# A routing table with 64 bytes for each entry, a smaller descriptor scratch, and the last wait on SyncE

## The chip, the core and the metric

The kernel runs on one core of one Trainium2 chip. The metric is the device time of one execution in microseconds (us). The kernel before was timed in three runs: 564.46, 564.67 and 567.79 us, median 564.67. One further execution was profiled; all rows below are from it.

## The reference

A block of a gated cross-attention model. `x` is [8, 256, 256] (eight batches of 256 tokens), the context is [8, 120, 256].

```python
x = x + tanh(g_xattn) * xattn(layernorm(x), ctx, w_q, w_kv, w_out, b_out)   # 16 heads of 64
x = x + tanh(g_ffn)   * ffn(layernorm(x), W1, W2, Wr)

def ffn(x, W1, W2, Wr):                      # 8 experts of 1024 hidden units
    probs = softmax(einsum('btd,ed->bte', x, Wr))
    topk_vals, topk_idx = top_k(probs, 2)
    gate = one_hot-weighted topk_vals / topk_vals.sum()
    h = silu(einsum('btd,efd->btef', x, W1));  y = einsum('btef,edf->bted', h, W2)
    return einsum('bte,bted->btd', gate, y)
```

Only the two experts that a token chooses count, so the kernel computes those alone. It computes in float16 with each operand split in a high and a low part.

## The kernel before

**Two phases share the engines.** The first phase takes the eight batches one after another through attention, second layer norm, router logits and routing. The second phase is the expert part: the 4096 pairs of token and expert are sorted by expert into 39 tiles of 128 rows (`TILES`), and each tile is gathered, multiplied by W1 and W2 of its expert, and added to the output. The first 13 tiles (`EARLY`) depend on the first five batches only, and tiles 0 to 9 are worked while the last batches are still in attention. Tiles 10 to 38 run in a loop of four tiles (`run_tiles`).

**What sets the order.** The order of each engine's work is written out by hand: each engine has a loop over `p` with a fixed list of calls (for GpSimd, called POOL in the rows, `scatter`, `p_low`, `find_rows`, `tile_gather`, `tile_add` and so on). Engines are in step through semaphores alone. A call that waits holds up everything behind it on its engine.

**The routing table.** `table` is a tensor in HBM with 129 blocks of 128 places. A place belongs to a slot of an expert, and holds the token's number and its gate: 2 float32, 8 bytes. It is used in four steps.

1. `constants` on POOL fills `pad` (a piece of SBUF inside the later `w2s`), and `store_pads` on SyncE (SP) copies it to all of `table` with 2 DMAs, so that unused places name a spare row.
2. Per batch, `route` on VectorE (DVE) writes `entry` and `slot`. `scatter` on POOL (L611) issues four indirect DMAs of 128 entries each; each entry is one 8-byte write to HBM at its slot. Eight batches make 32 of them. They count on `scattered`, which `find_rows` waits for, and `route` two batches later.
3. `find_rows` on POOL (L664) gathers 13 blocks after batch 4 and 26 blocks after batch 7 into `found`, one block a partition. `find_T` on TensorE (PE) transposes it, and `row_ids` on DVE makes `row_of` (which row each place of a tile takes) and the gates.
4. `tile_gather` (L678) fetches the 128 rows of a tile, and `tile_add` (L689) adds the tile's result `yt` to `out` with an indirect DMA that accumulates. An addition is issued only after the one before has landed (`y_added`).

**Other transfers.** SP loads the weights of a tile, `w1_tile` (in the rows `w_tile`), 1 MB each, at L454. `store_norm` stores the normalized rows `xn2`, and `norm2` on ScalarE (ACT, L876) waits for the store of the batch before.

**The end.** POOL's last line waits until all 39 additions have landed. Then every engine leaves the program through a closing step, which the rows show as DRAIN and semaphore instructions at L170. SP has only waited for the direct stores to `out`.

Of the kernel before, what the change touches and what calls it, by code (L numbers as in the profile page):

```python
# [36 lines left out]
BLOCKS = T // P  # L37

# [129 lines left out]
def build(nc, x, ctxT, wq, wkv, wo, bo, gx, gf, w1, w2, wr, out, xn2_dram, table, w1_dram):  # L168
    ctx = ExitStack()
    with ctx:  # L170
# [42 lines left out]
        found = sb("found", [P, 2 * P], F32)  # L213
# [55 lines left out]
        entry = [sb(f"entry{i}", [P, NT, TOPK, 2], F32, att) for i in range(2)]  # L269
# [11 lines left out]
        pad = raw[:, 14336:14336 + 2 * P].rearrange("p (r c) -> p r c", c=2)  # L281
# [116 lines left out]
        def _(sp):  # L398
# [69 lines left out]
            def store_pads(b):  # L468
                if b:
                    return  # L470
                sp.wait_ge(const_done, CONSTS)
                sp.dma_start(table_b[0:P, :], pad.rearrange("p r c -> p (r c)")).then_inc(table_in, 16)
                sp.dma_start(table_b[P:P + 1, :], pad[0:1].rearrange("p r c -> p (r c)")).then_inc(table_in, 16)
# [45 lines left out]
            sp.wait_ge(x2_out[1], 16 * (B + 1))  # L519

        @block.gpsimd
        def _(pool):
# [33 lines left out]
            def constants(b):  # L556
                if b:
# [15 lines left out]
                pool.iota(pad[:, :, 0], [[1, P]], base=T, channel_multiplier=0,  # L573
                          allow_small_or_imprecise_dtypes=True).then_inc(const_done, 1)
# [28 lines left out]
            def scatter(b, t):  # L603
                if not 0 <= b < B:
                    return
                if t == 0:
                    pool.wait_ge(route_done, b + 1)
                    if b == 0:
                        pool.wait_ge(table_in, 32)
                for k in range(TOPK):  # L610
                    pool.indirect_dma_start(out=table[:], out_offset=bass.IndirectOffsetOnAxis(slot[b % 2][:, t, k:k + 1], 0),  # L611
                                            in_=entry[b % 2][:, t, k, :], in_offset=None).then_inc(scattered[b % 2], 16)
# [140 lines left out]
            pool.wait_ge(y_added, 16 * TILES)  # L753

        @block.scalar
        def _(act):
# [156 lines left out]
            def split_high(q, i, k):  # L913
# [10 lines left out]
                else:  # L924
# [10 lines left out]
                    elif q < 7:  # L935
                        for j in range(2):
                            act.wait_ge(stats_done[j], 1)
                    else:
                        act.wait_ge(table_in, 32)
# [130 lines left out]
        def _(dve):  # L1070
# [10 lines left out]
            def constants(b):  # L1081
# [3 lines left out]
                nc.vector.tensor_copy(identb[:], ident[:]).then_inc(zero_done, 1)  # L1085
                chain.link(nc.vector.tensor_copy(base[0][:], seg[:]))
# [547 lines left out]
        def _(pe):  # L1634
# [244 lines left out]
            def find_T(b, late):  # L1879
# [5 lines left out]
                f = found[0:n, :].rearrange("t (r c) -> t r c", c=2)  # L1885
# [204 lines left out]
```

## Time and profile before

| what | value |
|---|---|
| median of three runs | 564.67 us |
| profiled execution, first to last instruction (span) | 560.1 us |
| median of the runs less that span | 4.6 us |
| PE, busy share of the span | 88% |
| DVE, ACT, POOL, busy share | 66%, 66%, 65% |
| DMA queues of SP and of POOL, share of 16 DMA engines | 46.7%, 9.5% |
| mean granted TensorE clock | 0.958 of full |

The profiled execution has no time of its own beside its span; the median of the runs stands 4.6 us above that span, which is launch and end outside the instructions. Busy shares are averages: until about 320 us four engines are busy together, after that PE is busy and the others about half of the time. "Idle before" is an engine's idle time ahead of an instruction, with what ended it; "issue" means that the profile shows nothing that it waited for.

### The profile page before, as it was taken

What the parts mean: (1) busy time and instruction counts of PE and PEld (TensorE: products, weight loads), DVE (VectorE), ACT (ScalarE), POOL (GpSimd) and SP (SyncE); (2) the same over time, 40 slices, a digit from 0 to 9 for tenths busy, and PEclk for the clock granted to TensorE, in tenths of its full rate; (3) what the DMA queues carried; (4) which work ended last, traced back from release to release, by engine and by line L of the source; (5) the groups of instructions that cost most, each with busy time, mean ns of one, the idle gap of its engine ahead of it and who ended that gap; (6) DMA issues with size and microseconds to landing.
All of it is one profiled execution on the core that took longest, in us unless ns stands there. A gap on an engine that the chain in (4) does not pass through costs nothing. (4 is left out here: it accounts for less than half of the span.)

```text
span 560.1 us, 17891 instructions
## 1 busy us (share of the span) xinstructions
PE 493.7 (88%) x6630; PEld 438.3 (78%) x6631; DVE 370.2 (66%) x856; ACT 371.3 (66%) x576; POOL 363.9 (65%) x372
## 2 busy tenths in 40 slices
PE   2869799998999999798788997699999999999990
PEld 2757688887888879687567886689898898988980
DVE  5899999898889899699996664343444444343430
ACT  1838999998999899789546674245455464645530
POOL 5466979798989998788978642533544436344531
PEclk9979889999999999999689998799999999999996
DMA  7922506173553625263438598766787877778421
GB/s 286 392 77 84 175 12 219 48 244 59 175 127 119 178 97 168 33 212 73 130 148 201 153 287 145 208 185 186 214 259 201 259 207 232 229 224 244 112 30 17
DMA packets 34846, 93.13 MB, mean 166 GB/s; under 512 B 4967, under 2 KB 24565, under 8 KB 27490
## 3 DMA queue, kind: packets, MB, share of 16 engines
q1 hardware_dynamic: 25634, 81.86, 46.7%
q0 software_dynamic: 8576, 10.30, 9.5%
q8 instruction: 40, 0.66, 0.6%
q10 hardware_dynamic: 576, 0.14, 0.1%
q14 instruction: 20, 0.16, 0.1%
HBM read 74.17 MB, written 18.12 MB: 165 GB/s over the span
## 5 line engine op out<-in xcount | busy, mean ns | idle before, releaser
L689 POOL DMA_INDIRECT out<-yt,row_of x39 | 65.0, 1667 | 115.3 <-DMA out<-yt,row_of 96.5
L1642 PE MATMUL st_bank<-xsT,w_tile 128*128 128x128 f16 x1872 | 114.4, 221 | 4.3 <-issue 3.3
L1480 DVE SCALAR_TENSOR_TENSOR hT<-hf,h_scale,hT 128x512 f16<-128x512 f32 x78 | 58.6, 754 | 88.1 <-ACT hT L974 88.1
L1642 PEld LDWEIGHTS st_bank<-xsT,w_tile 128*128 128x128 f16 x1872 | 109.2, 99 | 7.0 <-issue 5.4
L1642 PE MATMUL o_bank<-w2s,hT 128*128 x936 | 109.9, 274 | 1.2 <-DVE yt L1489 1.1
L1642 PEld LDWEIGHTS o_bank<-w2s,hT 128*128 128x128 f16 x936 | 90.4, 99 | 12.4 <-issue 1.6
L968 ACT ACTIVATE hf<-st_bank,z_scale 128x512 f32<-128x512 f32 x78 | 52.9, 679 | 47.9 <-PE st_bank L1642 40.4
L592 POOL TENSOR_TENSOR pT<-pT 120x512 f16<-120x512 f32 x64 | 77.3, 1221 | 8.0 <-ACT pT L842 7.7
L974 ACT ACTIVATE hT<-hf,h_scale 128x512 f16<-128x512 f32 x78 | 56.3, 722 | 13.1 <-ACT hf L968 4.5
L637 POOL TENSOR_SCALAR stage<-stage,upw 128x512 f32<-128x512 f32 x32 | 55.9, 1748 | 10.5 <-ACT w_hi L941 10.4
L841 ACT ACTIVATE pT<-st_bank,exp_bias,logit_scale 120x512 f32<-120x512 f32 x64 | 50.0, 781 | 12.1 <-PE st_bank L1858 11.6
L842 ACT ACTIVATE pT<-st_bank,exp_bias,logit_scale 120x512 f16<-120x512 f32 x64 | 50.1, 783 | 0.0
L949 ACT ACTIVATE xsT<-max_pair 128x256 f16<-128x256 f32 x39 | 14.9, 382 | 48.8 <-PE max_pair L1896 44.7
L678 POOL DMA_INDIRECT xg<-xn,row_of x39 | 39.8, 1019 | 11.3 <-issue 8.9
L1778 PE MATMUL j_bank<-wos,oT 128*128 128x256 f16 x384 | 45.4, 272 | 0.3 <-DVE oT L1179 0.3
L1642 PE MATMUL o_bank<-v,pT 120*128 120x65 f16 x768 | 35.1, 197 | 11.7 <-DVE o L1367 9.6
L1642 PEld LDWEIGHTS o_bank<-v,pT 120*128 120x128 f16 x768 | 30.3, 99 | 18.2 <-issue 16.2
L611 POOL DMA_INDIRECT table<-entry,slot x32 | 32.9, 1027 | 14.2 <-DVE entry L1324 7.2
L1642 PE MATMUL j_bank<-xnT,wqs 128*128 128x256 f16 x336 | 41.0, 273 | 0.3 <-DVE oT L1179 0.3
L1778 PEld LDWEIGHTS j_bank<-wos,oT 128*128 128x128 f16 x384 | 36.4, 98 | 4.5 <-DVE oT L1179 0.4
L1344 DVE TENSOR_REDUCE max_pair<-max_pair 128x8 f32<-128x960 f32 x32 | 37.0, 1155 | 0.0
L1489 DVE TENSOR_SCALAR yt<-o_bank,gate_y 128x256 f32<-128x256 f32 x39 | 18.9, 483 | 25.4 <-PE o_bank L1642 25.2
(217 smaller groups left out, 966.5 us busy)
## 6 DMA issues: line engine op xcount, KB each, us to landing
w_tile<-w_split SPq DMA_DIRECT2D x39, 1024.0 KB, 5.2
stage<-in_w SPq DMA_DIRECT2D x16, 1024.0 KB, 5.1
w_split<-w_hi SPq DMA_DIRECT2D x8, 512.0 KB, 2.8
w_split<-stage SPq DMA_DIRECT2D x8, 512.0 KB, 3.9
out<-x SPq DMA_DIRECT2D x17, 128.0 KB, 5.4
xin<-in_x SPq DMA_DIRECT2D x8, 256.0 KB, 4.7
w2s<-in_wkv SPq DMA_DIRECT2D x2, 1024.0 KB, 12.2
xres<-in_x SPq DMA_DIRECT2D x16, 128.0 KB
```

The source lines that it names most:

```text
L592: pool.tensor_tensor(pT[g % 2][:, 1, h, :], pT32[:, h, :], pT[g % 2][:, 0, h, :], ALU.subtract).then_inc(pT_low[h], 1)
L637: chain.link(pool.tensor_scalar(chunk, chunk, upw[q % 2][:, i:i + 1], None, ALU.mult))
L678: pool.indirect_dma_start(out=xg[t % XG][:], out_offset=None, in_=xn2_dram[0:rows], in_offset=bass.IndirectOffsetOnAxis(row_of[:, t:t + 1] ...
L689: pool.indirect_dma_start(out=out[0:rows], out_offset=bass.IndirectOffsetOnAxis(row_of[:, t:t + 1], 0), in_=yt[t % XG][:], in_offset=None, ...
L841: nc.scalar.activation(pT32[:, h, :], st_bank[h][0:M, :], ACT.Exp, bias=exp_bias[0:M], scale=logit_scale[0:M])
L842: nc.scalar.activation(pT[g % 2][:, 0, h, :], st_bank[h][0:M, :], ACT.Exp, bias=exp_bias[0:M], scale=logit_scale[0:M]).then_inc(exp_done[h ...
L968: nc.scalar.activation(hf[par][:, cols], z_bank[a][:], ACT.Silu, scale=z_scale[:, bass.ds(t, 1)]).then_inc(silu_done, 1)
L974: nc.scalar.activation(hT[par][:, 0, 4 * a:4 * a + 4, :], hf[par][:, cols].rearrange("p (c n) -> p c n", c=4), ACT.Copy, scale=h_scale[:, ...
L1344: ins = nc.vector.tensor_reduce(both[:, t].rearrange("p (h c) -> p h c", h=2), max_pair[:, :, 0:HP * M].rearrange("p h (c m) -> p h c m", ...
L1480: nc.vector.scalar_tensor_tensor(out=hT[par][:, 1, 4 * a:4 * a + 4, :], in0=hf[par][:, 512 * a:512 * a + 512].rearrange("p (c n) -> p c n" ...
L1642: ins = pe.matmul(out, lhs[i](a), rhs[i](c), start=(i == 0 and a + c == 0), stop=(i == n - 1 and a == 1))
L1778: ins = pe.matmul(dst[:, 0:D], oT[t][:, a, ic, :], wos[:, c, ic, :], start=(ic + a + c == 0), stop=(ic == IC - 1 and a == 1))
```

## The change

A place in `table` grows from 2 to 16 float32 (`ENTRY`), 64 bytes, of which 14 are zero. `entry`, `found` and `pad` grow with it. The scatter now writes whole places of 64 bytes, the two finds read blocks of 8 KB in place of 1 KB. `pad` is 64 rows of half a block (128 x 1024 float32), so `store_pads` needs six DMAs in place of two. Two memsets on DVE zero `entry` once. `pad` now also covers a part of expert 6's weights, so that ACT's split of these waits for the table's fill as that of expert 7 did. The SBUF that POOL's DMA descriptors get shrinks to 8192 bytes of each partition; before, no size was named. And the wait for the last addition moves from POOL's end to SP's end.

```diff
--- before.py
+++ after.py
@@ -35,6 +35,9 @@
 TOPK = 2
 TILES = TOPK * T // P + E - 1
 BLOCKS = T // P
+
+
+ENTRY = 16
 
 XG = 4
 
@@ -210,7 +213,7 @@
         row_of = sb("row_of", [P, TILES], I32)
         gate_y = sb("gate_y", [P, TILES], F32)
         expert_f = sb("expert_f", [P, TILES], F32)
-        found = sb("found", [P, 2 * P], F32)
+        found = sb("found", [P, ENTRY * P], F32)
         by_expert = sb("by_expert", [P, TILES - EARLY, E], F32)
         one_hot = sb("one_hot", [P, TILES - EARLY, E], F32)
 
@@ -266,7 +269,7 @@
         slot_m = chosen
         slot = [sb(f"slot{i}", [P, NT, TOPK], I32, att) for i in range(2)]
         ratio = sb("ratio", [P, 2, NT], F32, att)
-        entry = [sb(f"entry{i}", [P, NT, TOPK, 2], F32, att) for i in range(2)]
+        entry = [sb(f"entry{i}", [P, NT, TOPK, ENTRY], F32, att) for i in range(2)]
         att.close()
 
         xsT = [sb(f"xsT{i}", [P, 2, KC, P], F16) for i in range(2)]
@@ -278,7 +281,7 @@
 
 
         raw = w2s[:].rearrange("p e s c d -> p (e s c d)").bitcast(F32)
-        pad = raw[:, 14336:14336 + 2 * P].rearrange("p (r c) -> p r c", c=2)
+        pad = raw[:, 13824:13824 + ENTRY * P // 2].rearrange("p (r c) -> p r c", c=ENTRY)
         diag5 = raw[:, 14848:14848 + 5 * P // 2].bitcast(BF16).rearrange("p (i n) -> p i n", n=P)
         raw_k, raw_q, raw_v = (raw[:, 2048 * i:2048 * i + 2048].rearrange("p (k n) -> p k n", k=KC) for i in range(3))
         raw_o = raw[:, 6144:8192].rearrange("p (k n) -> p k n", k=IC)
@@ -469,8 +472,12 @@
                 if b:
                     return
                 sp.wait_ge(const_done, CONSTS)
-                sp.dma_start(table_b[0:P, :], pad.rearrange("p r c -> p (r c)")).then_inc(table_in, 16)
-                sp.dma_start(table_b[P:P + 1, :], pad[0:1].rearrange("p r c -> p (r c)")).then_inc(table_in, 16)
+                for h in range(2):
+                    to = table_b[:, h * ENTRY * P // 2:(h + 1) * ENTRY * P // 2]
+                    rows = pad[64 * h:64 * h + 64].rearrange("p r c -> p (r c)")
+                    for g in range(2):
+                        sp.dma_start(to[64 * g:64 * g + 64, :], rows).then_inc(table_in, 16)
+                    sp.dma_start(to[P:P + 1, :], rows[0:1]).then_inc(table_in, 16)
 
             sp.dma_start(xin[:], x_b[0]).then_inc(xin_in, 16)
             sp.dma_start(raw_q, wq).then_inc(raw_in[2], 16)
@@ -517,6 +524,7 @@
                 load_tile(B - 1, t)
             sp.wait_ge(x2_out[0], 16 * B)
             sp.wait_ge(x2_out[1], 16 * (B + 1))
+            sp.wait_ge(y_added, 16 * TILES)
 
         @block.gpsimd
         def _(pool):
@@ -570,8 +578,13 @@
                 pool.memset(sel[:], 0.0).then_inc(pool_chain, 1)
                 chain.n += 3
                 pool.wait_ge(pool_chain, chain.n)
-                pool.iota(pad[:, :, 0], [[1, P]], base=T, channel_multiplier=0,
-                          allow_small_or_imprecise_dtypes=True).then_inc(const_done, 1)
+                for h in range(2):
+                    ins = pool.iota(pad[64 * h:64 * h + 64, :, 0], [[1, 64]], base=T + 64 * h, channel_multiplier=0,
+                                    allow_small_or_imprecise_dtypes=True)
+                    if h == 0:
+                        chain.link(ins)
+                ins.then_inc(const_done, 1)
+                pool.wait_ge(const_done, CONSTS - 2)
                 pool.affine_select(out=upper[:], in_=upper[:], compare_op=ALU.is_gt, fill=0.0, base=0,
                                    pattern=[[1, P]], channel_multiplier=-1).then_inc(const_done, 1)
 
@@ -606,7 +619,7 @@
                 if t == 0:
                     pool.wait_ge(route_done, b + 1)
                     if b == 0:
-                        pool.wait_ge(table_in, 32)
+                        pool.wait_ge(table_in, 96)
                 for k in range(TOPK):
                     pool.indirect_dma_start(out=table[:], out_offset=bass.IndirectOffsetOnAxis(slot[b % 2][:, t, k:k + 1], 0),
                                             in_=entry[b % 2][:, t, k, :], in_offset=None).then_inc(scattered[b % 2], 16)
@@ -750,7 +763,6 @@
                 if t + XG < TILES:
                     gather(t + XG)
                 add(t)
-            pool.wait_ge(y_added, 16 * TILES)
 
         @block.scalar
         def _(act):
@@ -932,11 +944,11 @@
                             act.wait_ge(job_full, JOBS.fulled(name, 0))
                         if piece == 0:
                             act.wait_ge(ctx32_done, 2)
-                    elif q < 7:
+                    elif q < 6:
                         for j in range(2):
                             act.wait_ge(stats_done[j], 1)
                     else:
-                        act.wait_ge(table_in, 32)
+                        act.wait_ge(table_in, 96)
                     to, done = w2_part(q, 0, c, 1024), w2_high[k]
                 nc.scalar.activation(to, stage[i][:, c:c + 1024], ACT.Copy, scale=upw[q % 2][:, i:i + 1]).then_inc(done, 1)
 
@@ -1083,6 +1095,8 @@
                     return
                 dve.wait_ge(ident_done, IDENT)
                 nc.vector.tensor_copy(identb[:], ident[:]).then_inc(zero_done, 1)
+                for i in range(2):
+                    chain.link(nc.vector.memset(entry[i][:], 0.0))
                 chain.link(nc.vector.tensor_copy(base[0][:], seg[:]))
 
             def x_stats(b, part):
@@ -1882,7 +1896,7 @@
                 n = (EARLY, TILES - EARLY)[late]
                 dst = bank_free(FOUND[late], b)
                 pe.wait_ge(found_in, 16 * (1 + late))
-                f = found[0:n, :].rearrange("t (r c) -> t r c", c=2)
+                f = found[0:n, :].rearrange("t (r c) -> t r c", c=ENTRY)
                 pe.transpose(dst[:, 0:n], f[:, :, 0], ident[0:n, 0:n])
                 pe.transpose(dst[:, 64:64 + n], f[:, :, 1], ident[0:n, 0:n]).then_inc(job_full, 1)
 
@@ -2076,13 +2090,13 @@
         "w2": np.asarray(L0_ffn_W2).reshape(E, D, FC, P).transpose(0, 3, 2, 1),
         "wr": np.asarray(L0_ffn_Wr).reshape(E, KC, P).transpose(2, 1, 0),
     }
-    nc = bacc.Bacc("TRN2", target_bir_lowering=False, num_devices=1)
+    nc = bacc.Bacc("TRN2", target_bir_lowering=False, num_devices=1, dynamic_dma_scratch_size=8192)
     arrays = {f"in_{name}": np.ascontiguousarray(layout[name]) for name in INPUTS}
     args = [nc.dram_tensor(f"in_{name}", arrays[f"in_{name}"].shape, F32, kind="ExternalInput").ap() for name in INPUTS]
 
     out = nc.dram_tensor("out", (T + P, D), F32, kind="ExternalOutput").ap()
     xn2_dram = nc.dram_tensor("xn2", (T + P, D), F32, kind="Internal").ap()
-    table = nc.dram_tensor("table", (P * (P + 1), 2), F32, kind="Internal").ap()
+    table = nc.dram_tensor("table", (P * (P + 1), ENTRY), F32, kind="Internal").ap()
     w1_dram = nc.dram_tensor("w1_split", (E, P, 2, KC, DFF), F16, kind="Internal").ap()
     build(nc, *args, out, xn2_dram, table, w1_dram)
     result = run_bass_kernel_spmd(nc, [arrays], core_ids=[0])
```

The order of two engines changes at one place each. SP, at `store_pads`, early in the program (`w2s` is the tensor in which `pad` lies). Before:

```order
L490 DMA xn<-x_1 64x256 x2
L419 DMA xres<-in_x 128x256 x2
L472 DMA table<-w2s 128x256
L473 DMA table<-w2s 1x256
L412 DMA xin<-in_x 128x2x256
```

With the change:

```order
L497 DMA xn<-x_1 64x256 x2
L422 DMA xres<-in_x 128x256 x2
L479 DMA table<-w2s 64x1024 x2
L480 DMA table<-w2s 1x1024
L479 DMA table<-w2s 64x1024 x2
L480 DMA table<-w2s 1x1024
L415 DMA xin<-in_x 128x2x256
```

Six DMAs stand where two stood; the next one behind them, a load of `xin`, is the same.

DVE, at its `constants`, between the scales of the first weights (`pw`, `up`) and the first input (`xn2T`). Before:

```order
L1124 TENSOR_SCALAR pw<-pw 128x1 [waits dve_chain]
L1132 TENSOR_SCALAR up<-pw 128x1 [waits dve_chain]
L1085 CAST identb<-ident 128x128 [waits ident_done]
L1086 COPY base<-seg 128x8
L1200 TENSOR_SCALAR xn2T<-j_bank,up 128x512 [waits up_done2,job_full,dve_chain]
```

With the change:

```order
L1138 TENSOR_SCALAR pw<-pw 128x1 [waits dve_chain]
L1146 TENSOR_SCALAR up<-pw 128x1 [waits dve_chain]
L1097 CAST identb<-ident 128x128 [waits ident_done]
L1099 MEMSET entry 128x64
L1099 MEMSET entry 128x64 [waits dve_chain]
L1100 COPY base<-seg 128x8 [waits dve_chain]
L1214 TENSOR_SCALAR xn2T<-j_bank,up 128x512 [waits up_done2,job_full,dve_chain]
```

Two memsets, each waited for, are put in ahead of the copy to `base`.

## Rows read from the trace of the kernel before

**Rows 1.** Windows: stretch, busy us of PE, PEld, DVE, ACT, POOL, clock, DMA share, GB/s.

```profile
341.00:349.00 8.00, 4.67 (x58) 4.28 (x56) 2.72 (x8) 1.89 (x4) 0.00 (x0) 0.83 0.97 95
351.00:353.00 2.00, 2.00 (x34) 1.94 (x32) 1.27 (x3) 0.00 (x0) 0.64 (x1) 1.00 0.92 348
...
346.20:349.60 3.40, 2.74 (x20) 2.35 (x21) 0.00 (x0) 0.99 (x3) 0.00 (x0) 0.50 0.92 130
```

**Rows 2.** Timeline of POOL, 330 to 360 us: start, us, engine, line, operation, idle before.

```profile
332.73 1.25 POOL L611 DMA_INDIRECT table<-entry,slot  x1 [0.31 <-issue]
...
337.35 0.96 POOL L611 DMA_INDIRECT table<-entry,slot  x1 [0.30 <-issue]
338.61 1.59 POOL L689 DMA_INDIRECT out<-yt,row_of  x1 [0.30 <-issue]
352.36 1.97 POOL L689 DMA_INDIRECT out<-yt,row_of  x1 [12.16 <-DVE yt L1489]
```

**Rows 3.** DMA issues from 332 to 350 us, median us to landing last.

```profile
w_tile<-w_split SPq DMA_DIRECT2D x3, 1024.0 KB, 7.7
...
out<-yt,row_of POOLq DMA_INDIRECT x1, 13.0
```

**Rows 4.** DMA issues of the whole run, median us to landing last.

```profile
w_tile<-w_split SPq DMA_DIRECT2D x39, 1024.0 KB, 5.2
...
out<-yt,row_of POOLq DMA_INDIRECT x39, 4.8
```

**Rows 5.** Timeline of PE, 335 to 372 us.

```profile
341.42 2.12 PE L1642 MATMUL st_bank<-xsT,w_tile 128*128 128x128 f16 x35
346.86 1.57 PE L1642 MATMUL st_bank<-xsT,w_tile 128*128 128x128 f16 x13 [3.33 <-issue]
...
359.18 0.69 PE L1896 MATMUL max_pair<-ident,xg 128*128 128x128 f32 x2 [4.80 <-DMA xg<-xn,row_of]
...
366.79 0.30 PE L1886 MATMUL j_bank<-ident,found 26*128 26x26 f32 x1
```

**Rows 6.** Timeline of POOL: the first scatter of four batches.

```profile
157.55 1.08 POOL L611 DMA_INDIRECT table<-entry,slot  x1 [0.53 <-DVE entry L1324]
...
188.28 1.08 POOL L611 DMA_INDIRECT table<-entry,slot  x1 [0.17 <-issue]
...
219.60 1.08 POOL L611 DMA_INDIRECT table<-entry,slot  x1 [0.53 <-DVE entry L1324]
...
253.66 1.08 POOL L611 DMA_INDIRECT table<-entry,slot  x1 [0.53 <-DVE entry L1324]
```

**Rows 7.** Timeline of PE, two places in attention.

```profile
139.93 0.63 PE L1791 MATMUL j_bank<-ident,xn 128*128 128x128 f32 x4 [0.93 <-ACT xn L876]
...
227.89 1.50 PE L1642 MATMUL j_bank<-wkvs,ctxs 128*120 128x512 f16 x6 [1.36 <-issue]
```

**Rows 8.** Timeline of ACT at 139 us.

```profile
139.19 0.60 ACT L876 ACTIVATE xn<-x,ln_b 128x256 f32<-128x256 f32 x1 [1.76 <-DMA xn<-xn]
```

**Rows 9.** Timeline of all engines, 546 to 560 us: its last row.

```profile
548.11 1.54 POOL L689 DMA_INDIRECT out<-yt,row_of  x1 [2.83 <-DMA out<-yt,row_of]
```

**Rows 10.** Line 170, the closing step: operation, count: ns min/median/max, first and last start.

```profile
L170 POOLq EVENT_SEMAPHORE  x2: 17/17/17, 559.9 to 560.0; - x2
...
L170 POOLq COMPARE_BRANCH  x1: 41/41/41, 551.9 to 551.9; - x1
L170 POOLq DRAIN  x1: 7780/7780/7780, 552.1 to 552.1; - x1
```

**Rows 11.** Timeline of POOL, 9 to 22 us.

```profile
9.27 0.31 POOL L569 MEMSET w2s<- 128x256 f32 x1
...
21.49 0.25 POOL L546 TENSOR_SCALAR ln_a<-mv 128x4 f32<-128x4 f32 x1 [8.10 <-DVE mv L1102]
```

**Rows 12.** Timeline of DVE, 0 to 3 us.

```profile
1.48 0.27 DVE L1079 MEMSET x<- 128x256 f32 x1
```

**Rows 13.** Timeline of SP, 26 to 41 us.

```profile
26.74 0.43 SPq L472 DMA_DIRECT2D table<-w2s  x1
...
40.34 0.40 SPq L412 DMA_DIRECT2D xin<-in_x  x1
```

**Rows 14.** Line 664, the two finds: operation and landing.

```profile
L664 POOL DMA_INDIRECT found<-table,blk x2: 917/977/1037, 273.4 to 360.4; - x2
...
DMA to landing us min/median/max: 2.8/2.9/2.9
```

## The prediction

> **What bounds the kernel now.** I read the views in this order: the slices of clock and DMA, the windows around the slices where PE drops, the timelines of POOL and PE there, the DMA issues with their landings, the same for the attention phase, and last the closing step.
>
> In the expert loop PE is the bound and nothing of it is edited. What matters are places where PE stops. The dearest lies between 341 and 360 us. POOL issues the last four scatters from 332.7 to 338.3 us and an addition behind them at 338.61 [rows 2]. That addition lands after 13.0 us, while the median of all 39 is 4.8, and weight loads issued in this stretch take 7.7 us against 5.2 [rows 3, 4]. In those 8 us the DMA engines are occupied (share 0.97) but move 95 GB/s; a little later, with no scatter in flight, a share of 0.92 moves 348 GB/s [rows 1]. So something holds the engines without moving bytes. The scatters are the only new thing in flight: 4 x 128 writes of 8 bytes, 4 KB in all. I read from this that a write of 8 bytes to HBM is dear, some (13.0 - 4.8) / 4 = 2.05 us of every DMA engine per scatter, or 0.26 us for each of the eight writes that an engine gets if 128 are dealt to 16.
>
> PE pays in the same stretch: it stops for 3.33 us in the middle of a product, between two matmuls that wait for nothing that the profile shows ("issue"), and its clock is at half speed from 346.2 to 349.6 [rows 5, 1]. A stop there, with DMA moving almost nothing, looks like late instructions, which come by DMA too. The later gap of 4.80 us before the transposes of gathered rows [rows 5] is another matter: its gather is queued on POOL behind the addition at 352.36, which waited for DVE's `yt` [rows 2].
>
> **The scatter with 64 bytes.** What is removed is the stalls, if a full place of 64 bytes is written without what makes 8 bytes dear. Nothing in the trace writes 64 bytes to HBM, so I bound it. From below: nothing improves, 0. From above: every loss that follows a scatter closely.
> - The stop in the last batch 3.33 us, and half of the 3.4 us at half clock, 1.7 [rows 5, 1].
> - Fourth batch: the first scatters of batches start at 157.55, 188.28, 219.60 and 253.66 [rows 6], periods of 30.7, 31.3 and 34.1 us. The long one holds a PE stop marked "issue" just after that batch's scatters [rows 7]. Against the shortest it loses 3.4 us.
> - First batch: PE waits 0.93 us for ACT's norm, which waited 1.76 us for the store of `xn` that was issued among the scatters [rows 7, 8].
>
> The ends are 0 and 3.33 + 1.7 + 3.4 + 0.93 = 9.4 us. I take 60% of the upper, 5.6 us: the four engines are nearly equally busy in attention, so the next one's wait takes a part, and the 4.80 us gap stays, since it belongs to POOL's order. The bytes are no cost: 32 scatters carry 8 KB each in place of 1.
>
> The Trainium skill speaks against this (DMA: Bandwidth & Descriptors, Specifications): transfers below 512 B make the DMA engine read, modify and write. By that rule 64 bytes are as dear as 8, the 5.6 us fall away, and the sum is rival 1's. The same notes ask elsewhere only for buffers aligned to 32 bytes to avoid it (Collectives: The Full Stack, Rules for kernel authors), and by that the gain would stand. The rows show 8 bytes to be dear and cannot part the two.
>
> **The last wait on SP.** POOL's last addition is issued from 548.11 to 549.65 us [rows 9]. POOL then waits for its landing until about 552, and only then begins its closing DRAIN, 7.78 us long, which ends the program: all other engines are already waiting [rows 10]. Without the wait the DRAIN can begin at about 549.7, 2.4 us earlier, and SP, idle by then, waits beside it. If the DRAIN's length is a fixed piece of work, the end comes 2.4 us earlier. Bounds: 0 if it cannot get on before the addition has landed; 2.4 + 7.78 / 2 = 6.3 us if its length also goes with the scratch, which is halved or so (the size before isn't in the rows). I take 2.4, since only the start is sure to move.
>
> **The smaller scratch.** At most six indirect DMAs are in flight at once, 338 to 350 us [rows 2, 3], and I see no row where POOL waits for room. I take 0. If POOL had to wait once for an addition to land before it could go on, that is up to 4.8 us [rows 4], mostly hidden, since an addition waits for the one before anyway.
>
> **The small edits.**
> - DVE: two memsets of 128 x 64, each waited for. One of 128 x 256 takes 0.27 us [rows 12], so about 0.15 each with its wait, 0.3 us, on the path to the first input. Cost 0.3. Uncovered in full.
> - POOL: `pad` grows from 256 to 1024 columns; 0.31 us becomes at most 1.2 [rows 11]. With a second iota and two waits some 1.3 us. POOL idles 8.10 us behind it [rows 11]. Cost 0; were the cover gone, 1.3.
> - SP: four more issues of 0.43 us [rows 13], 1.7 us; the next one behind waits until 40.34 anyway [rows 13]. The 1 MB that they fill moves in about 5 us, as a tile's weights do [rows 4], in that same gap. Cost 0.
> - The finds: blocks of 8 KB, 104 and 208 KB in all, in place of 13 and 26. They land after 2.9 us now [rows 14]; I allow 1 us more. The late one is issued at 360.4 and read at 366.79 [rows 14, 5], so 3.5 us are to spare. Cost 0.
> - ACT's new wait for the table's fill stands late in the attention phase, long after 32 us. Cost 0.
>
> **Sum.** -5.6 - 2.4 + 0.3 = -7.7 us against the profiled span: 560.1 becomes 552.4. The median of the runs stands 4.6 us above that span, so 564.67 - 7.7 = 557.0 us.
>
> **Rivals.**
> 1. *64 bytes are as dear as 8.* For: an engine that deals with each small write by itself pays for the write, not for its size, and 0.26 us each fits that. Against: neighbouring 8-byte places share a stretch of 64 bytes, full ones do not. Then only -2.4 + 0.3 remain: 562.6 us. Chance 0.23.
> 2. *The DMA engines come free, but PE hardly gains.* For: four engines share the bound in attention, and the 4.80 us gap is fed by POOL. Against: the stop of 3.33 us lies in a PE-bound stretch. A gain of 1.5 there: 564.67 - 1.5 - 2.4 + 0.3 = 561.1 us. Chance 0.15.
> 3. *The closing DRAIN shortens with the scratch.* For: the same instruction is long only on POOL, the engine that has issued through the scratch [rows 10]. Against: no row shows what it does. 557.0 - 3.9 = 553.1 us. Chance 0.12.
> 4. *Slower: each write now takes a stretch of its own in memory.* The tokens of a batch that chose one expert take adjacent slots, so eight writes of 8 bytes now fall into one stretch of 64 bytes. If memory pays by the stretch, a spread over eight times as many doubles the 2.05 us per scatter. In the last batch that is 4 x 2.05 = 8.2 us more in front of PE, with no gain at the other places: 564.67 + 8.2 - 2.1 = 570.8 us. It decides once a scatter costs over 2.05 + 2.1 / 4 = 2.6 us. Against: the fill of full places should be the easier case. Chance 0.05.
>
> **Chances.** The forecast itself has 0.45. A change of 1% is 5.6 us, about what can be told from none. Faster by over 1% (below 559.0): 0.40 of the forecast's 0.45 (a good part of its spread lies below), all of rival 3, 0.04 of rival 2: 0.56. Slower by over 1%: rival 4 and mishaps, 0.05. The rest 0.39. The range runs from 549.5 (the upper bound of 9.4 with a part of the shorter DRAIN) to 564.5 (rival 1 with nothing won at the end). The forecast's own range is 553 to 560.
>
> **What would show it.** In 341 to 349 us the DMA engines should move over 200 GB/s at a share above 0.9, or have a low share; the addition behind the last scatters should land in under 6 us; PE's stop inside a product should be gone. POOL's DRAIN at the closing line should begin within 0.3 us of the last addition's issue; its length tells rival 3. If the same windows still show DMA shares near 1 at 100 GB/s, rival 1 holds; if the addition lands later than 13 us, rival 4. The prediction is wrong in its main term if those stalls vanish and PE's busy time per stretch stays as it was.

## The result: 564.6 us before, 542.7 us after

The changed kernel takes 542.66 us (median of 6 runs, 536.78 to 543.89); the kernel before, on the same chip, 564.57 us (6 runs, 561.68 to 567.79). The ratio is 0.9616, 95% interval 0.9572 to 0.9661. The gain is 22 us where 7.7 were forecast, and the time lies below the range. The profiled execution took 542.3 us with a span of 539.4. Some executions of a kernel fall in a slower state of the chip, and the medians and ratios of the studies below leave these out, three strays of 1315, 1705 and 1827 us among them.

Setting the two profiled executions against each other at five instructions that both have, I find where the spans' 20.7 us are:

| stretch | before, us | after, us | difference |
|---|---|---|---|
| start to the first scatter of the first batch | 125.56 | 124.32 | -1.2 |
| from there to the fifth batch's first scatter | 128.10 | 123.65 | -4.4 |
| from there to the last batch's first scatter | 79.07 | 78.10 | -1.0 |
| from there to the ninth addition | 47.19 | 40.82 | -6.4 |
| from there to the issue of the last addition | 168.19 | 168.03 | -0.2 |
| from there to the end of the span | 11.99 | 4.48 | -7.5 |

**The last batch.** Windows of the changed kernel, columns as in [rows 1]; the first three hold the scatters and what follows, the fourth is a stretch at half clock, the last is from the last batch's first scatter to the ninth addition:

```profile
326.00:334.00 8.00, 8.00 (x111) 7.58 (x110) 6.71 (x23) 5.34 (x10) 5.91 (x5) 1.00 0.73 224
334.00:342.00 8.00, 8.00 (x110) 7.60 (x108) 4.66 (x10) 3.72 (x7) 4.51 (x4) 1.00 0.84 211
342.00:352.00 10.00, 7.30 (x106) 6.83 (x103) 5.16 (x12) 5.69 (x9) 2.52 (x2) 1.00 0.84 267
352.40:355.80 3.40, 3.40 (x30) 3.07 (x28) 1.49 (x5) 0.69 (x1) 1.48 (x1) 0.50 0.85 251
...
326.10:366.90 40.80, 37.07 (x473) 34.46 (x472) 21.26 (x56) 19.69 (x34) 19.00 (x16) 0.96 0.73 210
```

and the like stretch of the kernel before:

```profile
332.70:380.00 47.30, 38.14 (x457) 34.75 (x455) 20.36 (x55) 19.31 (x32) 19.48 (x16) 0.89 0.78 174
```

In the 16 us from 326 the DMA engines move 211 to 224 GB/s at a share of 0.73 to 0.84, where they moved 95 at 0.97, and PE is busy throughout. Over the whole stretch PE's idle time falls from 9.2 us (47.3 less 38.14 busy) to 3.7 (40.8 less 37.07), and its busy time by 1.1 as less of it falls at half clock: 6.5 us together.

POOL's timeline there, after (compare [rows 2]; columns: start, us, engine, line, operation, idle before it and what ended that):

```profile
326.07 1.03 POOL L624 DMA_INDIRECT table<-entry,slot  x1 [0.30 <-issue]
...
330.35 0.96 POOL L624 DMA_INDIRECT table<-entry,slot  x1 [0.30 <-issue]
331.61 1.59 POOL L702 DMA_INDIRECT out<-yt,row_of  x1 [0.30 <-issue]
336.19 1.57 POOL L702 DMA_INDIRECT out<-yt,row_of  x1 [2.99 <-DVE yt L1503]
338.07 1.00 POOL L691 DMA_INDIRECT xg<-xn,row_of  x1 [0.30 <-issue]
...
343.15 1.60 POOL L702 DMA_INDIRECT out<-yt,row_of  x1 [1.53 <-DMA out<-yt,row_of]
345.06 0.91 POOL L677 DMA_INDIRECT found<-table,blk  x1 [0.30 <-issue]
352.31 1.57 POOL L702 DMA_INDIRECT out<-yt,row_of  x1 [6.33 <-DMA out<-yt,row_of]
```

The addition behind the scatters, issued at 331.61, lands after 3.8 us (the DMA view of a window around it) where it took 13.0 [rows 3], so the next one goes 4.6 us behind it and not 13.8. PE's timeline after has neither the stop inside a product nor the gap before the gathered rows [rows 5]:

```profile
331.79 1.06 PE L1656 MATMUL st_bank<-xsT,w_tile 128*128 128x128 f16 x16
332.69 2.78 PE L1656 MATMUL o_bank<-w2s,hT 128*128 x24
335.31 0.38 PE L1910 MATMUL max_pair<-ident,xg 128*128 128x128 f32 x2
335.52 2.84 PE L1656 MATMUL st_bank<-xsT,w_tile 128*128 128x128 f16 x48
338.20 2.78 PE L1656 MATMUL o_bank<-w2s,hT 128*128 x24
...
351.89 0.26 PE L1900 MATMUL j_bank<-ident,found 26*128 26x26 f32 x1 [2.70 <-DMA found<-table,blk]
```

The last row is a new cost: PE waits 2.70 us for the late find, and just behind that stop its clock is at half for 3.4 us (the fourth window above). The finds' line (landing last) shows why PE waits, against 2.8 to 2.9 us before [rows 14]:

```profile
L677 POOL DMA_INDIRECT found<-table,blk x2: 914/976/1037, 267.7 to 345.1; - x2
...
DMA to landing us min/median/max: 3.8/5.2/6.7
```

**Attention.** The first scatters of batches 2 to 5 start at even steps of 30.7 to 31.3 us, where the step from 219.60 took 34.1 [rows 6]:

```profile
155.22 1.08 POOL L624 DMA_INDIRECT table<-entry,slot  x1 [0.18 <-issue]
...
185.96 1.08 POOL L624 DMA_INDIRECT table<-entry,slot  x1 [0.18 <-issue]
...
217.24 1.08 POOL L624 DMA_INDIRECT table<-entry,slot  x1 [0.53 <-DVE entry L1338]
...
247.97 1.08 POOL L624 DMA_INDIRECT table<-entry,slot  x1 [0.17 <-issue]
```

**The end.** The last addition and the closing step, after (compare [rows 9, 10]):

```profile
534.92 1.54 POOL L702 DMA_INDIRECT out<-yt,row_of  x1 [3.04 <-DMA out<-yt,row_of]
```

```profile
L173 POOLq EVENT_SEMAPHORE  x2: 17/17/17, 539.2 to 539.3; - x2
...
L173 POOLq DRAIN  x1: 4481/4481/4481, 534.7 to 534.7; - x1
L173 SPq COMPARE_BRANCH  x1: 41/41/41, 538.8 to 538.8; - x1
```

The DRAIN now stands beside the issue and its landing and ends 2.7 us behind the issue's end (536.46); before it ended 10.2 us behind it (549.65 to 559.9). The trace's event for the landing is at 538.68, and the DRAIN ends 0.49 us behind it; in all eleven traces of kernels with both edits of the end it ends 0.49 to 0.50 us behind the landing. So what is left of it then ends with the last transfer.

**The small edits.** The pad costs POOL 0.95 us in place of 0.31, and the idle time behind it shrinks from 8.10 to 6.37 [rows 11]: no cost, as forecast.

```profile
10.25 0.95 POOL L577 MEMSET w2s<- 128x1024 f32 x1
...
21.81 0.25 POOL L554 TENSOR_SCALAR ln_a<-mv 128x4 f32<-128x4 f32 x1 [6.37 <-DVE mv L1116]
```

DVE's two memsets stand at 17 us, and `xn2T` behind them starts at 17.52 in place of 17.20. Their size was right: 0.30 us for both.

```profile
16.98 0.30 DVE L1099 MEMSET entry<- 128x64 f32 x2
```

### The profile page after: what moved, and what is told of

The parts are those of the page before. It is cut to its first block, busy times and chain, and to the rows that moved or that the text cites. A ratio compares the mean times of both kernels' runs of the same rounds, so it can differ in the third digit from the quotient of the medians.

```text
span 539.4 us, 17897 instructions
## 1 busy us (share of the span) xinstructions
PE 485.3 (90%) x6630; PEld 433.5 (80%) x6631; DVE 369.4 (68%) x858; ACT 371.0 (69%) x576; POOL 367.4 (68%) x373
## 4 chain that ended last, share of the span: by engine, by line
DMA 34%; PE 31%; DVE 12%; POOL 10%; issue 9%; ACT 3%; POOLq 0%; SPq 0%; ACTq 0%; DVEq 0%
DMA out<-yt,row_of 32%; PE j_bank L1656 8%; PE o_bank L1656 5%; PE j_bank L1792 4%; POOL pT L605 3%; PE st_bank L1656 3%; POOL stage L650 3%; PE st_bank L1869 2%; PE max_pair L1848 2%; PE j_bank L1752 2%; DMA stage<-in_w 2%; DMA w2s<-in_wq 1%; POOL table L624 1%; PE j_bank L1662 1%; POOL w2s L654 1%
## 5 line engine op out<-in xcount | busy, mean ns | idle before, releaser
L980 ACT ACTIVATE hf<-st_bank,z_scale 128x512 f32<-128x512 f32 x78 | 53.0, 679 | 47.3 <-PE st_bank L1656 41.3
L1656 PEld LDWEIGHTS j_bank<-xnT,wqs 128*128 128x128 f16 x336 | 31.8, 98 | 4.7 <-DVE oT L1193 0.5
```

Source lines behind the costliest of these rows:

```text
L980: nc.scalar.activation(hf[par][:, cols], z_bank[a][:], ACT.Silu, scale=z_scale[:, bass.ds(t, 1)]).then_inc(silu_done, 1)
L1656: ins = pe.matmul(out, lhs[i](a), rhs[i](c), start=(i == 0 and a + c == 0), stop=(i == n - 1 and a == 1))
```

## The experiments

The kernels of one study ran on one chip, and each study on another chip than the one of the result: times are compared within a study, beside the kernel before there. Its median was 563.7 us (10 runs) in the first, 564.0 (7) in the second, 557.6 (7) in the third and 553.6 (5) in the fourth. Single executions of it spread over 9 to 17 us on those chips, so a difference of 3 us between two profiles tells little; lengths of single instructions tell more.

### First study: the parts of the end

**end_wait_b**: the kernel before, with the last wait moved from POOL to SP.

```diff
             for t in range(LISTED - 1, TILES):
...
-            pool.wait_ge(y_added, 16 * TILES)
...
             sp.wait_ge(x2_out[1], 16 * (B + 1))
+            sp.wait_ge(y_added, 16 * TILES)
```

> The kernel before with only the wait for the last addition moved from POOL to SP; table and scratch as before. In the changed kernel POOL's closing DRAIN took 4.48 us and the program ended 2.9 us after the last addition's issue, in place of 10.5 us. Theory W (the DRAIN is work that overlaps the landing once the wait is elsewhere, and its length does not go with the scratch): DRAIN begins with the last issue, the program ends about 2.9 us after it, -7.5 us, about 557 us. Theory S (its length goes with the scratch): the DRAIN stays near 7.8 us and only starts earlier, -2.4 us, about 562 us.

**end_scratch_b**: the kernel before, with the scratch alone.

```diff
-    nc = bacc.Bacc("TRN2", target_bir_lowering=False, num_devices=1)
+    nc = bacc.Bacc("TRN2", target_bir_lowering=False, num_devices=1, dynamic_dma_scratch_size=8192)
```

> The kernel before with only the scratch for POOL's descriptors at 8192 bytes; the wait stays on POOL. Theory W: nothing changes, DRAIN 7.8 us, 564.6 us. Theory S: the DRAIN takes about half, 3.9 us, 560.7 us. If the smaller scratch costs waits on POOL, the spans of its indirect DMAs grow and the body of the program gets longer.

**end_both_b**: both of these edits.

> The kernel before with both: scratch 8192 and the wait on SP; table as before. Both theories expect the end of the changed kernel, 2.9 us from the last issue to the end, so about 557 us. What the changed kernel has beyond this (542.7 us, so some 14 us) is the table's.

**table_pool_wait_b**: the changed kernel, with the wait back on POOL.

```diff
-            sp.wait_ge(y_added, 16 * TILES)
...
+            pool.wait_ge(y_added, 16 * TILES)
```

> The changed kernel with the wait for the last addition put back on POOL (scratch stays 8192, places of 64 bytes). Theory W: DRAIN of 7.8 us after the landing, the end is 7.5 us later than in the changed kernel, about 550 us. Theory S: DRAIN of 3.9 us after the landing, about 3.5 us later, 546 us. Against the run with the smaller scratch alone this gives the table's part, about 14 us.

Measured: 563.55 us (ratio 0.9997, interval 0.9927 to 1.0068), 561.66 (1.0005, 0.9931 to 1.008), 560.68 (0.9944, 0.9891 to 0.9997) and 554.43 (0.9891, 0.9751 to 1.0031). By the times, no part of the end shows by itself, and both together give 3 us, by the interval 0.2 to 6.1. The closing step shows more in single traces. Rows of that step's line (operation, count: ns, first and last start), first the wait on SP alone:

```profile
L170 POOLq EVENT_SEMAPHORE  x2: 17/17/17, 562.6 to 562.6; - x2
L170 POOLq DRAIN  x1: 9552/9552/9552, 553.0 to 553.0; - x1
```

then the scratch alone:

```profile
L170 POOLq EVENT_SEMAPHORE  x2: 17/17/17, 566.3 to 566.4; - x2
L170 POOLq COMPARE_BRANCH  x1: 41/41/41, 564.4 to 564.4; - x1
L170 POOLq DRAIN  x1: 1696/1696/1696, 564.6 to 564.6; - x1
```

and both edits:

```profile
L170 POOLq DRAIN  x1: 4420/4420/4420, 557.0 to 557.0; - x1
```

With the wait on SP the last addition's issue ends at 554.72 and the DRAIN at 562.55, 7.8 us later: that fits the same 7.8 us of work, begun as the issue ends. The span ends 8.0 us behind the issue's end, where before it was 10.45: 2.4 us gained, as forecast. With the smaller scratch alone the DRAIN takes 1.70 us in place of 7.78, 6.1 us gained (table_pool_wait_b shows 1696 ns again). Both together end 2.9 us behind the issue's end, 7.5 us gained: what is left is the landing, and SP's part adds 1.5 to the scratch's 6. These 7.5 us lie outside the interval of end_both_b's times here, and inside that of end_both_c in the third study; why the times of this study show less of it stays open.

### Second study: what about a scatter is dear

**after_again** is the changed kernel, to be read beside the next three.

> The changed kernel itself, on the chip of this comparison, so that the three variants of it beside it can be read against it. Theory P (the place of 64 bytes takes stalls out of the DMA engines): 0.96 of the kernel before, no gap of TensorE over 1 us among the products of the last batch, and the addition behind the last four scatters (the fourth of the run) issued about 16 us earlier than before; the last addition issued some 13 us earlier and the end 3 us behind that issue. Theory Q (the body's gain of some 13 us was made up by the one execution that I read): the last addition is issued within 4 us of where it was, and the ratio is 0.985, which is the end alone.

**place_32**: 32 bytes for each entry.

```diff
-ENTRY = 16
+ENTRY = 8
```

> The changed kernel with 32 bytes for each entry in place of 64. Theory P32 (what is dear is a stretch shared by two writes, of 32 bytes at most): as the changed kernel, and the last find's blocks of 4 KB instead of 8 land about 2 us sooner, so 0 to 2 us faster. Theory P64 (the stretch is 64 bytes): half or more of the body's gain is lost, 5 to 12 us slower than the changed kernel, with gaps of TensorE of 2 to 5 us near 340 us back.

**write_8**: places of 64 bytes, but only the entry's 8 bytes written.

```diff
-                    pool.indirect_dma_start(out=table[:], out_offset=bass.IndirectOffsetOnAxis(slot[b % 2][:, t, k:k + 1], 0),
-                                            in_=entry[b % 2][:, t, k, :], in_offset=None).then_inc(scattered[b % 2], 16)
+                    pool.indirect_dma_start(out=table.rearrange("n (s c) -> (n s) c", c=2), out_offset=bass.IndirectOffsetOnAxis(slot[b % 2][:, t, k:k + 1], 0),
+                                            in_=entry[b % 2][:, t, k, 0:2], in_offset=None).then_inc(scattered[b % 2], 16)
...
+                chain.link(nc.vector.tensor_scalar(slot_e[:], slot_e[:], 8.0, None, ALU.mult))
```

> Places of 64 bytes, but each entry's write is of 8 bytes as before (the slot numbers are multiplied by 8 in one more VectorE instruction of 27 ns or so in each batch). The rest of a place keeps what the pad gave it. Theory own place (what was dear is that several writes fell into one stretch): as the changed kernel within 1.5 us. Theory size of the write (a write of 8 bytes is dear wherever it lands, since the rest of its stretch is read first): the stalls come back, the body 8 to 13 us longer than the changed kernel's.

**write_32**: the same with c=8, in_=...0:8 and a factor of 2: the first half of each place is written.

> Places of 64 bytes, of which each entry's write fills the first 32. Theory own place: as the changed kernel within 1.5 us. Theory size of the write with a unit of 32 bytes: the same. Theory size of the write with a unit of 64 bytes: the stalls come back, the body 8 to 13 us longer.

Measured: after_again 553.52 us (ratio to before 0.9793, 0.9721 to 0.9866), place_32 553.66 (0.9835, 0.975 to 0.992), write_8 551.79 (0.9787, 0.9719 to 0.9855), write_32 551.18 (0.9751, 0.9673 to 0.983). The four can't be told apart. POOL in write_8, the last scatter and what follows it:

```profile
337.33 0.96 POOL L624 DMA_INDIRECT table<-entry,slot  x1 [0.30 <-issue]
338.59 1.71 POOL L702 DMA_INDIRECT out<-yt,row_of  x1 [0.30 <-issue]
344.81 1.57 POOL L702 DMA_INDIRECT out<-yt,row_of  x1 [4.50 <-DVE yt L1504]
```

The addition behind the scatters lands after 3.7 to 4.0 us in all four. So a write of 8 bytes is cheap where it has 64 bytes to itself: neither the size of a write nor a partly filled place is what costs. By the rule that I weighed (the Trainium skill, DMA: Bandwidth & Descriptors, Specifications) all of these writes are small and would be dear alike; here they are not. The alignment of buffers to 32 bytes that the Trainium skill asks for (Collectives: The Full Stack, Rules for kernel authors) is in agreement with place_32. One question stays open: in all the cheap layouts each write also starts at a multiple of 32 bytes and the writes are spread over more memory, and no run has lone writes that start elsewhere. So what is shown is the layout; that sharing is the reason, and not the start or the spread, is only argued.

### Third study: where the table acts

**before_again** and **after_c** are the two kernels unchanged, **end_both_c** is end_both_b's kernel again.

> The kernel before, unchanged, to have its trace from the same chip as the three beside it. Theory L (the table gains only in the last batch): attention periods of 31.7 us as in the changed kernel on this chip, and a stop of the DMA engines behind the last four scatters, with the addition behind them landing after 11 to 13 us. Theory A (the table also gains in each attention batch): periods 0.5 us or more longer than those of the changed kernel here.

> The kernel before with the smaller scratch and SyncE's wait, and so everything of the change that acts at the end, without the table. Against the kernel before on this chip: 7.5 us less (ratio 0.987) if the end's gain stays whole; its body ends where that of the kernel before ends, within 3 us.

> The changed kernel on the same chip as the kernel before and the end alone. Theory L: the body gains 8 to 11 us over those two, all of it between the last scatters and the sixth or seventh addition, and the time is 0.965 to 0.98 of before's. Theory A: more than 3 us of the gain lie before the last four scatters.

**place_16**: 16 bytes for each entry.

```diff
-ENTRY = 16
+ENTRY = 4
```

> The changed kernel with 16 bytes for each entry: two neighbouring entries share 32 bytes, four share 64. If what is dear is a stretch of 32 bytes shared by two writes: the addition behind the last four scatters lands after 6 to 13 us and most of the body's gain is gone, 4 to 10 us slower than the changed kernel. If what is dear is a stretch of 16 bytes or less: as the changed kernel, landing in under 5 us.

Measured: before_again 556.24 us (0.9988, 0.9934 to 1.0043), end_both_c 551.05 (0.9883, 0.9772 to 0.9994), after_c 541.63 (0.9724, 0.9629 to 0.982), place_16 545.83 (0.9849, 0.9735 to 0.9962). From the end alone to the whole change is 9.4 us here. In the first study it was 6.2, and there the wait on POOL took 1.5 back, so 7.7. That is the table's gain, 8 to 9 us, in medians of four to nine runs.

The attention periods are 30.7 to 31.0 us in all four profiles: Theory L holds for the steady batches. Windows of 8 us that begin 3 to 4 us behind the last scatter's issue, of before_again and, below it, of place_16 (columns as in [rows 1]):

```profile
334.60:342.60 8.00, 8.00 (x119) 7.71 (x117) 3.87 (x11) 3.38 (x6) 0.00 (x0) 1.00 0.96 129
```

```profile
332.60:340.60 8.00, 8.00 (x119) 7.69 (x117) 4.77 (x13) 3.39 (x6) 0.33 (x1) 1.00 0.93 240
```

In before_again PE runs through the stretch and pays afterwards, at the gathered rows. In end_both_c it stops inside a product and again at the rows. PE's timeline of the first, and of the second:

```profile
351.72 0.69 PE L1896 MATMUL max_pair<-ident,xg 128*128 128x128 f32 x2 [8.55 <-DMA xg<-xn,row_of]
```

```profile
341.03 1.42 PE L1642 MATMUL st_bank<-xsT,w_tile 128*128 128x128 f16 x13 [2.70 <-issue]
351.87 0.69 PE L1896 MATMUL max_pair<-ident,xg 128*128 128x128 f32 x2 [2.99 <-DMA xg<-xn,row_of]
```

From the first issue of the last batch's four scatters to their last landing the traces give 12.9 to 16.1 us in the eight profiles with 8-byte places, 11.9 with 16 bytes, 5.9 to 6.0 with 32 bytes and with 64 in the first and second study, and 9.1 with 64 in the result's profile and after_c, where weight loads run beside them. On one chip that is 12.9 to 16.1 against 6.0 in the first study, and 14.1 and 14.6 against 11.9 and 9.1 in the third. With 16 bytes the addition behind lands after 9.9 us, inside the 6 to 13 expected of a shared 32 bytes, but after_c has 7.4. Its time is 4.2 us above the changed kernel's, with intervals that overlap: a part of the price, and not settled how much.

### Fourth study: doubled scatters, and other scratches

**twice_8** is end_both_b's kernel with each scatter issued a second time, into a second table that nobody reads; **twice_64** is the same for the changed kernel. The waits on `scattered` count twice as much.

```diff
+                    pool.indirect_dma_start(out=table2[:], out_offset=bass.IndirectOffsetOnAxis(slot[b % 2][:, t, k:k + 1], 0),
+                                            in_=entry[b % 2][:, t, k, :], in_offset=None).then_inc(scattered[b % 2], 16)
```

> The kernel before with the smaller scratch and SyncE's wait, and every scatter issued a second time, into a second table that nobody reads. Theory M (many writes of 8 bytes into one stretch of memory are dear, about 2 us of all DMA engines for each scatter): the eight scatters of the last batch take 18 to 25 us from the first issue to the last landing, and the time is 6 to 12 us above the end alone (551 to 561 us in the studies before this one, according to the chip). Theory O (a scatter's dearness is its issue and its descriptors): twice_64 shows the same.

> The changed kernel with every scatter issued a second time, into a second table of 64-byte places that nobody reads. Theory M: what is added is POOL's issue, 1.28 us for each of four more scatters in front of the waiting addition, 5.1 us of POOL, of which TensorE feels 0 to 3; the last scatter lands within 4 us of its issue. Theory O: as for 8 bytes, 6 to 12 us more than the changed kernel.

**scratch_4096** and **scratch_12288** are end_scratch_b's kernel with these sizes.

> The kernel before with a scratch of 4096. Theory size (the closing DRAIN goes with the scratch: 7.8 us with the size before, 1.7 with 8192): 1 to 1.7 us. Theory rest (it goes with what is left to clear since the scratch was last gone through): some other length between 0 and 4 us, and POOL waits for room in front of a scatter or an addition in the last batch, 1 to 5 us.

> The kernel before with a scratch of 12288. Theory size: halfway, a DRAIN of 4 to 5.5 us. Theory rest: any other length, 1.7 or 7.8 us among them.

Measured: twice_8 594.49 us (ratio to before 1.0686, 1.056 to 1.0811), twice_64 589.54 (1.0649, 1.0542 to 1.0755), one run each of scratch_4096, 550.86, and scratch_12288, 558.5. Both doubled kernels missed: I expected the 64-byte one to gain 0 to 3 us of TensorE time, and it is some 36 us above before. The attention batches pay, and in the same way. PE in twice_64 and in twice_8:

```profile
140.19 0.81 PE L1658 MATMUL o_bank<-v,pT 120*128 120x65 f16 x12 [5.14 <-issue]
```

```profile
143.19 0.82 PE L1644 MATMUL o_bank<-v,pT 120*128 120x65 f16 x12 [5.13 <-issue]
```

Four more issues of 1.28 us, 5.1 us, stand in front of POOL's part of `pT`, and PE waits 5.1 us in each of the first four batches. The period rises to 37.5 us (37.6 to 38.1 in twice_8) from 31; a part of the rest is the clock, 0.91 in twice_64's window from 161.1 to 198.5 and 1.00 in the like one of the result. So POOL's queue, which is busy for 29 of those 31 us, is on the path of attention, whatever a scatter's bytes. The widths differ only at the last batch: from the first issue to the last landing twice_8 takes 19.4 us and twice_64 13.3, of which the eight issues are 9.8. That fits the price of shared places, at the lower end of the 18 to 25 us expected.

The DRAIN with 4096 and with 12288:

```profile
L170 POOLq DRAIN  x1: 1287/1287/1287, 547.2 to 547.2; - x1
```

```profile
L170 POOLq DRAIN  x1: 3656/3656/3656, 551.6 to 551.6; - x1
```

It takes 1.29, 1.70 and 3.66 us with 4096, 8192 and 12288, and 7.78 in both profiles with the size before. It grows with the scratch, but not in proportion: the first step costs 0.4 us and the next 2.0. The two new sizes were run once each. My halfway value, 4 to 5.5 us, missed. What the DRAIN does I can't tell from this; no wait of POOL for room shows with 4096 in the last batch.

## Why the prediction failed, step by step

**The last wait on SP, forecast 2.4 us, and the smaller scratch, forecast 0.** The first held: 2.4 us by end_wait_b. The second failed: the DRAIN shortens by 6.1 us. This was rival 3, which I gave 0.12 and priced at half the DRAIN, 3.9 us. The ground that I had against it (no row shows what the DRAIN does) was no evidence against it, since it holds against a fixed length as well, and the fact in its favour was in [rows 10]: only POOL's closing DRAIN is long. The end gives 7.5 us in place of 2.4, since the two overlap at the landing.

**The scatter, forecast 5.6 us.** What held is that 8-byte places are dear and wider ones are not. The price was put in the wrong place, though: I took it for 2.05 us of every DMA engine per scatter. The queues of the DMA view before, 332 to 350 us (packets, MB, share of the 16 engines), show otherwise; q0 is POOL's and holds the scatters, q1 is SP's with the weight loads:

```profile
q1 hardware_dynamic: 371, 2.64, 87.6%
q0 software_dynamic: 364, 0.31, 8.6%
```

By the packet records the four scatters are 64 packets of 15 ns, 1.0 us in all. The 8 KB packets of SP's queue have a median of 0.32 us, but average 0.82 and reach 3.70 in the 18.6 us from 332.73; in the 18.3 us from 326.07 of the changed kernel the median is 0.31, the mean 0.39 and the longest 1.40. So the scatters slow the other transfers and do not fill the engines themselves. What slows them, no run shows. Nor does any show what PE's stop of 3.33 us waited for: the one record of an instruction load near it runs from 340.95 to 341.93, before the stop at 343.5, which neither shows late instructions nor rules them out.

In the sum two things were off. One is the share of 60%. On the result's chip the two attention losses of [rows 6, 7] came back whole: 4.4 us by the table of stretches, against my 3.4 and 0.93. The long fourth period is no steady loss, though. Of eight profiles with 8-byte places three show it (34.1 to 35.4 us), and none of the eight with wider places does. So what it is worth depends on the execution.

The other failed step is one sentence: "the 4.80 us gap stays, since it belongs to POOL's order". I had read from [rows 2] that the addition at 352.36 waited for DVE's `yt`. Three rows of `yt` on DVE's timeline before show otherwise:

```profile
336.13 0.48 DVE L1489 TENSOR_SCALAR yt<-o_bank,gate_y 128x256 f32<-128x256 f32 x1
...
341.40 0.48 DVE L1489 TENSOR_SCALAR yt<-o_bank,gate_y 128x256 f32<-128x256 f32 x1 [0.26 <-PE o_bank L1642]
...
351.73 0.48 DVE L1489 TENSOR_SCALAR yt<-o_bank,gate_y 128x256 f32<-128x256 f32 x1 [6.12 <-PE o_bank L1642]
```

Additions and `yt` come in the order of the tiles, 39 of each. The addition at 352.36 is the fourth, and the fourth `yt` is the row of 336.13, done at 336.61. The row of 351.73 is the sixth, and merely ended at nearly the time at which the addition of 338.61 landed, 351.6 (338.61 and 13.0). The addition waited for that landing, and the gather behind it, and PE's 4.80 us behind that gather, were the scatters' doing as well. Adding it would have put the last batch's loss at 5.0 + 4.8 = 9.8 us; 6.4 came back, since 2.70 are lost again at the find. Within the scatter's term this is the larger failed step: 4.8 us were taken to stay, for a reason that the rows refute.

**The finds, forecast 0.** I had 3.5 us to spare and allowed 1 us for the larger blocks. The late one lands after 6.7 us and is read 6.8 us behind its issue: 2.70 us lost. In four other profiles of the changed layouts (after_again, place_32, write_8, after_c) it lands after 4.5 to 6.8 us and is read later, with no gap. Blocks of 1 KB are no safeguard: in the seven other profiles with these the late find lands after 3.5 to 5.9 us, and three of them lose 0.95 to 2.3 us. So what the larger blocks cost is not settled; the 2.8 us of the one trace that I read was the lowest of eight.

**The memsets, 0.3, and the pad, 0**, held in size. SP's issues and ACT's wait show no cost, and nothing tests them by themselves. The first 1.2 us of the table of stretches I can't explain: among the other profiles the first scatter starts anywhere from 122.7 to 126.6 us with 8-byte places and from 123.1 to 125.1 with wider ones.

**Rivals.** Rival 1 (64 bytes as dear as 8) falls by the result and by write_8. Rival 2's ground, that attention's bound is shared and won't give, holds in the steady batches (periods of 30.7 to 31.0 us with either layout in the third study), but the places that did give lay elsewhere. Rival 4 falls too: spreading writes over eight times the memory made them cheaper.

**What of the 22 us is general.** In the two later studies that ran the changed kernel itself its ratios to before are 0.9793 and 0.9724, with intervals up to 0.9866 and 0.982, against 0.9616 here. End (7.5, by the closing step) and table (8 to 9) give 15 to 17 us; the medians give 16.0 in the third study and 10.5 in the second. The other 5 or so of the result belong to the chip or to the executions of it; why, stays open. No variant beats the changed kernel by more than the spread.

## What to carry to other kernels

When a scatter writes small records, look whether neighbours share 32 bytes: give each record 32 bytes of its own, beginning at a multiple of 32, which need not be filled, and test the layout apart from the write's size. Look at the packets of the other queues too: they can be what a small write slows. Ask how long the closing DRAIN on POOL is, and try a smaller scratch before anything else at the end. When a row names the releaser of a wait on two semaphores, count which item of the named engine was really needed (the fourth addition, the fourth `yt`), and put the transfer's landing beside it.

## What the runs showed of the hardware

- 8-byte writes into places of their own: the addition behind 4 x 128 of them lands after 4.0 us (write_8). With eight neighbours in 64 bytes: 8.3 to 14.2 us in eight profiles.
- The scatters' own packets are short, 15 ns before; SP's 8 KB packets beside them average 0.82 us and reach 3.70, against 0.39 and 1.40 with 64-byte places.
- POOL's closing DRAIN: 1.29, 1.70, 3.66 us with a scratch of 4096, 8192, 12288 and 7.78 with the size before, the two that were seen twice with the wait on POOL (7780 and 1696 ns) the same to the nanosecond. With the wait on SP and 8192 bytes it ends 0.5 us behind the last landing.
- A scatter of 128 entries costs POOL 1.28 us to issue, whatever its width, and in attention PE pays it in full: a wait of 5.1 us for four, and a period longer by more than that.
